# Scores of an attention layer from two-part float32r operands in two halves of the array's rows, in a schedule of sixteen like steps

## The reference

```python
x = x + 0.5 * ffn(layernorm(x))
x = x + attention(layernorm(x))
x = x + 0.5 * ffn(layernorm(x))

# attention: 16 heads of 16 columns, over the 512 rows of a batch
q, k, v = x @ Wq + bq, x @ Wk + bk, x @ Wv + bv
q, k = rope(q), rope(k)
scores = einsum('bhqd,bhkd->bhqk', qh, kh) / sqrt(16)
out = einsum('bhqk,bhkd->bhqd', softmax(scores), vh)
return out @ W0 + b0

# ffn: base layer, eight autoencoders (256 -> 64 -> 256), and the adapter
# (256 -> 64 -> 256) that belongs to the autoencoder with the smallest loss on this batch
h = relu(x @ W_enc[n] + b_enc[n]); recon = h @ W_dec[n] + b_dec[n]
top1 = argmin_n mean((recon - x) ** 2)
return x @ W_base + b_base + adapter[top1](x)
```

## Time and profile before

| | us |
|---|---|
| median of 3 runs | 1968.64 (1968.19 to 1973.37) |
| profiled execution | 1970.23 |
| its span | 1968.4 |
| TensorE busy | 1812.3 (92%) |
| VectorE busy | 1270.6 (65%) |
| ScalarE busy | 986.5 (50%) |
| GpSimd busy | 503.9 (26%) |

### The profile page before, as it was taken

The page is one execution under the profiler, slowest core; times in us unless marked ns, Lnnn a source line. Parts: engine busy times, 40 slices in busy tenths (PEclk is TensorE's granted clock), DMA queues, the critical chain, the costliest instruction groups (busy, mean ns, idle before and its releaser), DMA issues.

```text
span 1968.4 us, 26397 instructions
## 1 busy us (share of the span) xinstructions
PE 1812.3 (92%) x9128; PEld 988.0 (50%) x9128; DVE 1270.6 (65%) x2795; ACT 986.5 (50%) x1954; POOL 503.9 (26%) x663
## 2 busy tenths in 40 slices
PE   6598999999999999999999999999999999998885
PEld 5343545454554645455454545545454554545244
DVE  5476776667666766666676676666667666674631
ACT  1245564545555455555545555564555545454541
POOL 1404132141412214141221414122141412213101
PEclk9698999999999999999999999999999999999897
DMA  4513215060320506032050603206050320505000
GB/s 110 91 17 70 39 28 91 12 108 6 64 51 26 94 12 108 4 71 46 27 93 12 108 4 70 47 21 98 12 108 2 67 52 20 100 1 105 4 12 11
DMA packets 96781, 99.40 MB, mean 50 GB/s; under 512 B 19975, under 2 KB 88328, under 8 KB 96520
## 3 DMA queue, kind: packets, MB, share of 16 engines
q1 hardware_dynamic: 93896, 97.19, 26.7%
q10 hardware_dynamic: 2752, 0.54, 0.2%
HBM read 63.54 MB, written 33.55 MB: 49 GB/s over the span
## 4 chain that ended last, share of the span: by engine, by line
PE 61%; DVE 12%; DMA 12%; ACT 4%; SPq 4%; issue 4%; POOL 2%; POOLq 0%; ACTq 0%; DVEq 0%
PE ps L514 10%; PE ps L502 9%; PE ps L581 8%; PE ps L490 8%; DMA scratch<-parts 7%; DVE mx L832 6%; PE ps L560 6%; SPq L475 4%; PE ps L569 4%; DMA out_dram<-x 4%; PE ps L618 3%; PE ps L636 3%; ACT pr L716 2%; PE ps L621 2%; PE ps L681 2%
## 5 line engine op out<-in xcount | busy, mean ns | idle before, releaser
L832 DVE TENSOR_REDUCE mx<-ps 128x1 f32<-128x512 f32 x1024 | 653.5, 682 | 230.6 <-PE ps L490 229.6
L716 ACT ACTIVATE pr<-ps 128x512 f32<-128x512 f32 x1024 | 555.8, 598 | 292.0 <-PE ps L502 291.5
L490 PE MATMUL ps<-stack 96*128 96x512 bf16 x1024 | 326.1, 387 | 27.1 <-DVE mx L832 23.7
L502 PE MATMUL ps<-stack 98*128 98x512 bf16 x1024 | 323.2, 386 | 20.0 <-ACT pr L716 9.5
L514 PE MATMUL ps<-pr,va 128*32 128x512 f32 x2048 | 274.3, 608 | 4.6 <-ACT pr L716 4.6
L502 PEld LDWEIGHTS ps<-stack 98*128 98x128 bf16 x1024 | 77.5, 100 | 273.5 <-ACT pr L716 174.3
L771 ACT ACTIVATE h<-ps,benc 128x512 f32<-128x512 f32 x128 | 88.0, 687 | 216.2 <-PE ps L560 216.2
L490 PEld LDWEIGHTS ps<-stack 96*128 96x128 bf16 x1024 | 97.8, 98 | 187.8 <-DVE mx L832 91.7
L884 DVE SCALAR_TENSOR_TENSOR ps<-ps,wb,h 128x512 f32<-128x512 f32 x128 | 96.7, 755 | 140.7 <-PE ps L569 140.7
L1029 POOL TENSOR_SCALAR rs<-mv 128x4 f32<-128x4 f32 x48 | 11.6, 242 | 608.3 <-DVE mv L852 602.6
L581 PE MATMUL ps<-xh,w_dh 128*128 128x512 f32 x256 | 124.4, 486 | 9.2 <-DVE ps L884 6.7
(11 more groups left out here) (155 smaller groups left out, 2971.0 us busy)
## 6 DMA issues: line engine op xcount, KB each, us to landing
stack<-scratch SPq DMA_DIRECT2D x384, 128.0 KB, 4.5
scratch<-parts SPq DMA_DIRECT2D x64, 384.0 KB, 5.6
xin<-in_L_attn_x_dram SPq DMA_DIRECT2D x16, 512.0 KB, 3.8
out_dram<-x SPq DMA_DIRECT2D x16, 512.0 KB, 6.1
stack<-wu_mT SPq DMA_DIRECT2D x128, 4.0 KB, 1.7
cst<-in_const_dram SPq DMA_DIRECT2D x1, 1024.0 KB
raw<-in_L_ffn_W_dec_dram ACTq DMA_DIRECT2D x1, 512.0 KB, 5.7
pr<-in_L_ffn_W_enc_dram SPq DMA_DIRECT2D x2, 256.0 KB, 7.6
```

The source lines that it names most:

```text
L490: pe.matmul(bank1[:, t % 2, :], stack[b.odd][0][0:KB, hd, 128 * t:128 * t + 128], stack[b.odd][1][0:KB, hd, :], start=True, stop=True).the ...
L502: pe.matmul(bank2[:, a % 2, :], stack[b.odd][1][:, 4 * g + a, 128 * t:128 * t + 128], stack[b.odd][0][:, 4 * g + a, :], start=True, stop=T ...
L716: act.activation(pr[:, n % 2, a, :], bank2[:, a % 2, :], ACT.Exp, scale=SCALE).then_inc(ex_done.sem, 1)
L832: dve.tensor_reduce(mx[:, hd // 4 % 2, e:e + 1], bank1[:, t % 2, :], AX.X, ALU.max).then_inc(mx_done.sem, 1)
```

## The change

- **Operands.** q and k are split in two float32r parts (high and low) in place of three bf16 parts. A head has three blocks of 16 rows in place of six (48 rows, 50 with the maxima). The GpSimd step for the rest and the ScalarE step for the middle part are gone.
- **Two halves of the array.** Even heads stand in partitions 0 to 49 of the stack, odd heads in 64 to 113. A score matmul then uses one half of the array's rows only. The four score matmuls of a half step (two of line 552 for the maxima, two of line 565 with the maxima subtracted) are issued in turn: half 0, half 1, half 1, half 0.
- **One stack.** The stack is held once. A new step, lift, reads the scratch back: 12 transfers at a time, for two of the four blocks, once the batch before has no more use for that half of the heads. High and low parts go to the scratch apart (put_high, put_low).
- **Sixteen like steps.** An iteration has 16 steps of two halves, each with both kinds of scores; the second scores and pv of a batch run over into the next iteration (LAG = 5). Each half step has about one piece of dense work. The end of the second feed-forward (dn, up, store) stands in the iteration after the next. x1 is held three times, va twice; the squares, the whole transposed input and oT have buffers of their own. gr isn't cut in two any more. en steps stand one in a half step, where first two of them stood together.

```diff
-BLOCKS = 6
+BLOCKS = 3
 KB = BLOCKS * HD
-Q_PARTS = (0, 0, 1, 0, 2, 1)
-K_PARTS = (0, 1, 0, 2, 0, 1)
+HALF = 64
+Q_PARTS = (0, 1, 0)
+K_PARTS = (0, 0, 1)
...
+STEPS = 16
+LAG = 5
...
+    def attention(s, half):
+
+        shifted = (i, s - LAG) if s >= LAG else (p, s - LAG + STEPS)
...
+        if now or shifted: step("ss", i if now else None, s, shifted, half)
...
+    for t in range(2 * STEPS):
+        attention(t // 2, t % 2)
+        if old and t == 0: step("mt", p, 3)
+        if now and t in (8, 16, 24): step("mt", i, t // 8 - 1)
+        if now and t == 10:
+            step("lift", i, 2)
+            step("lift", i, 3)
+        if old: second_ffn(t)
+        if older: end_ffn(t)
...
-        parts = [sb(f"parts{k}", [128, 3, S], BF16) for k in range(2)]
-        stack = [[sb(f"stack{o}{a}", [KB + 2, H, S], BF16) for a in range(2)] for o in range(2)]
+        parts = [sb(f"parts{k}", [128, S], FR) for k in range(3)]
+        stack = [sb(f"stack{a}", [128, H // 2, S], FR) for a in range(2)]
...
+            def spread(b, k, part):
+
+                for j, p in enumerate((Q_PARTS, K_PARTS)[k % 2]):
+                    if p == part:
+                        for e in range(2):
+                            sp.dma_start(stack[k % 2][HALF * e + HD * j:HALF * e + HD * j + HD, 4 * (k // 2):4 * (k // 2) + 4, :].bitcast(F32),
+                                         scratch[b.odd][k].rearrange("(h e) d a n -> e d h a n", e=2)[e, :, :, part, :])\
+                                .then_inc(stacked[k].sem, 16)
+
+            def lift(b, k):
+
+                sp.wait_ge(*ex_done.at(b - 1, H * T * (k // 2 + 1) // 2 - 1))
+                sp.sem_inc(passed, 1)
+                sp.wait_ge(*hi_put[k].at(b, 0))
+                spread(b, k, 0)
+                sp.wait_ge(*lo_put[k].at(b, 0))
+                spread(b, k, 1)
...
+            def maximum_scores(b, m, e):
+
+                p, t = divmod(m, T)
...
+                q = slice(HALF * e, HALF * e + KB)
+                pe.wait_ge(*mx_done.at(b, 2 * m + e - 2))
+                pe.matmul(bank1[:, e, :], stack[0][q, p, 128 * t:128 * t + 128], stack[1][q, p, :],
+                          start=True, stop=True).then_inc(s1_full.sem, 1)
+
+            def shifted_scores(b, n, half, x):
...
+                p, e = 2 * g + half, 1 - x
+                q = slice(HALF * e, HALF * e + KB + 2)
+                pe.wait_ge(*ex_done.at(b, 4 * n + 2 * half + x - 2))
+                pe.matmul(bank2[:, x, :], stack[1][q, p, 128 * t:128 * t + 128], stack[0][q, p, :],
+                          start=True, stop=True).then_inc(s2_full.sem, 1)
+
+            def scores(b, s, shifted, half):
+
+                for x in range(2):
+                    if b:
+                        maximum_scores(b, 2 * s + half, x)
+                    if shifted:
+                        shifted_scores(*shifted, half, x)
```

More of the change, by code:

```diff
@@ L113, in step @@
             do[name](*args)
-    def dense(s, half):
-        at = (s, half)
-        if new and at == (0, 0):
+    def attention(s, half):
+        shifted = (i, s - LAG) if s >= LAG else (p, s - LAG + STEPS)
+        if not 0 <= shifted[0].number < B:
+            shifted = None
+        if now or shifted: step("ss", i if now else None, s, shifted, half)
+        if shifted: step("s2", *shifted, half)
+        if now:
+            step("s1", i, s, half)
+            if s % 4 == 3 and half: step("ms", i, s // 4)
+        for b, m in ((i, s), (p, s + STEPS)):
+            if not 0 <= b.number < B:
+                continue
+            if LAG < m <= LAG + STEPS and half == (m < LAG + STEPS): step("pv", b, m - LAG - 1)
@@ new lines, in end_ffn @@
+    def end_ffn(t):
+        if t == 3: step("dn", pp, 1)
+        if t == 9: step("up", pp, 1, 0)
+        if t == 10:
+            step("up", pp, 1, 1)
+            step("store", pp)
+    for t in range(2 * STEPS):
[7 more added lines that the diff above has]
+        if older: end_ffn(t)
+        if new:
+            first_ffn(t)
+            queries(t)
@@ L210, in dense @@
-        if at == (23, 1):
-            if now: step("ot", i)
-            if load:
+            if t == 31:
                 step("tr", i + 2, 0, 0)
                 step("tr", i + 2, 0, 1)
-    for s in range(24):
-        for half in (0, 1):
-            if now:
-                if 5 <= s < 21: step("s2", i, s - 5, half)
-                if s < 16: step("s1", i, s, half)
-                if s in (3, 7, 11, 15) and half: step("ms", i, s // 4)
-                if 6 <= s < 22 and half == (s < 21): step("pv", i, s - 6)
-            dense(s, half)
@@ L232, in enter, with walk @@
             do[name](first, *args)
-def walk(engine, do):
-    def one(i, number, odd):
-        schedule(do, Batch(number, odd), now=0 <= i < B, old=1 <= i <= B, new=i + 1 < B, load=i + 2 < B)
-    def known(i):
-        one(i, i, i)
-    for i in range(-1, B + 1):
-        known(i)
+def walk(do):
+    for number in range(-1, B + 2):
+        schedule(do, number)
 def macaron(nc, x_in, Wq, bq, Wk, bk, Wv, bv, W0, b0, W_base, b_base, W_enc, b_enc, W_dec, b_dec, W_down, b_down,
@@ L478, in _, with put_high @@
-            walk(sp, dict(load=load, store=store, mt=maxima, ro3=stack_up))
-            sp.wait_ge(*stored.at(Batch(B - 1, 1), 0))
+                for e in range(2):
+                    sp.dma_start(stack[0][HALF * e + KB:HALF * e + KB + 2, 2 * g:2 * g + 2, :]
+                                 .rearrange("n a (t k) -> n (a t) k", k=128).bitcast(F32),
+                                 mT[16 * e:16 * e + 16, g % 2, :].bitcast(F32)).then_inc(mq_done[g % 2].sem, 16)
+            def put_high(b, k):
+                sp.wait_ge(*hi_done.at(b, k))
+                sp.dma_start(scratch[b.odd][k][:, :, 0, :].rearrange("h d n -> (h d) n"), parts[HI_SLOT[k]][:].bitcast(F32))\
+                    .then_inc(hi_put[k].sem, 16)
@@ L481, in _ @@
+            def lift(b, k):
[5 more added lines that the diff above has]
+                spread(b, k, 1)
+            walk(dict(load=load, store=store, mt=maxima, ro2=put_high, ro3=put_low, lift=lift))
+            sp.wait_ge(*stored.at(Batch(B - 1), 0))
         @block.tensor
         def _(pe):
-            def s1(b, hd, half):
-                if half == 0 and hd % 8 == 0:
-                    pe.wait_ge(*stacked[2 * (hd // 8)].at(b, 0))
-                    pe.wait_ge(*stacked[2 * (hd // 8) + 1].at(b, 0))
-                for t in range(2 * half, 2 * half + 2):
-                    pe.wait_ge(*mx_done.at(b, T * hd + t - 2))
-                    pe.matmul(bank1[:, t % 2, :], stack[b.odd][0][0:KB, hd, 128 * t:128 * t + 128],
-                              stack[b.odd][1][0:KB, hd, :], start=True, stop=True).then_inc(s1_full.sem, 1)
@@ L683, in out_project @@
                 last.then_inc(op_full.sem, 1)
-            do = dict(s1=s1, s2=s2, pv=pv, mt=maxima, tr=transposed, en=encode, gr=gram, cost=cost, dn=down,
+            do = dict(ss=scores, pv=pv, mt=maxima, tr=transposed, en=encode, gr=gram, cost=cost, dn=down,
                           up=up, qk=project, va=values, nt=natural, ot=out_transposed, op=out_project)
```

465 lines of the change are left out of this document (233 added, 232 removed), and 3 rows, old and new, of the table QK.

## The result

The changed kernel takes 2094.24 us (median of 4 runs, 2090.33 to 2098.35); the kernel before took 1968.41 us beside it. The ratio is 1.0636, with a 95% interval of 1.0601 to 1.067: 6.4% slower, where 1826 us were forecast. The execution that was profiled took 2090.33 us, with a span of 2088.5.

The account below looks back on a forecast made before the run. TensorE was taken as the bound. Cheaper scores (7.4 us) and fewer stalls (1.5) save 8.9 us per iteration, 142 us over 16, from the profiled 1970.2 to 1828, or 1826 for the median; range 1750 to 1915.

Parts of the forecast that it names:

- What scores cost afterwards: TensorE's four score matmuls per half step: 0.64 us in place of 0.87, gaining 7.4 us per iteration (1.9 to 12.8).
- each change of mode empties the array: Rival: two drains and exposed loads make each half step's score group 1.04 us, 2031 us in all; chance 0.06.
- What stalls become: TensorE's idle time per iteration: 4.0 us go and 2.5 come, so -1.5 us (between +2.5 and -4.0).
- One wait grows: TensorE's wait at half step 0's encoder, behind the transposes of batch i+2, becomes about 2.5 us.
- The clock: Granted clock below full in mid-span, from sparser TensorE use, would make the forecast wrong altogether; not in the sum.
- The one stack: SyncE's twelve reads into the stack take 9.8 us of a near 20 us window, costing nothing; rival of lateness, chance 0.05.
- The first rival: Row halves don't run together: a half step's four score matmuls take 1.10 us, 2063 us in all; chance 0.14.
- Another engine takes over: Rival: VectorE's row maxima or ScalarE's exponents hold TensorE back, stalls grow by 6 us, 1946 us; chance 0.07.

Follow-up runs that it names:

- the run with three moves: Changed kernel with batch i+2's transposes, first feed-forward's dn and up, and second feed-forward's encoder steps moved to other half steps: 1949.93 us, ratio 0.9892.
- the run in one half: Changed kernel with the odd heads' scores replaced by the even heads', so all score matmuls use one row half: 2231.24 us, ratio 1.1323.
- the filler: Changed kernel plus unused float32r matmuls, 18 ahead of dn's wait and 12 ahead of the first q projection's: 2059.09 us, ratio 1.0432.
- the earlier transposes: Changed kernel with the transposes of batch i+2 in half steps 29 and 30 in place of 31 and 0: 2036.91 us, ratio 1.0329.
- all rows: Changed kernel with each score matmul over all 128 rows, both heads together, so scores are not those of a head: 2079.44 us, ratio 1.0552.
- the better order: Changed kernel with transposes, dn, up and second feed-forward's encoder steps moved: 1949.93 us with half-row scores, 1984.27 us with scores over all 128 rows.

## Why the prediction was wrong

The forecast was a period of 105.7 us, 8.9 less than before; it was 123.0, 8.4 more. Three terms make up the 8.4, from the window of the changed kernel and the full-clock iteration of the run with three moves: TensorE's work at the full clock, 106.3 less 110.3, is -3.9 us; the lower clock adds 110.6 less 106.3, +4.3; idle time adds +8.1. For the first point below, pv in the timeline of the kernel before, with a float32r matmul behind it:

```profile
1043.24 0.61 PE L502 MATMUL ps<-stack 98*128 98x512 bf16 x2
...
1044.21 1.07 PE L514 MATMUL ps<-pr,va 128*32 128x512 f32 x8
1045.21 0.49 PE L560 MATMUL ps<-xh,w_eh 128*128 128x512 f32 x1
1045.54 0.40 PE L560 MATMUL ps<-xh,w_el 128*128 128x512 f32 x1
```

- **What scores cost afterwards: failed.** The step was "For going in and out I have 0 below (bf16 to float32r costs nothing in rows 3) and 0.34 above ... I take the middle, 0.17". It is 0.40, outside my bounds. The two turns of 0.47 and the side-by-side halves were right (the run in one half). Pv's 0.22 was no fair row: its loads have 32 columns, and I read it where bf16 stands behind it. Where a float32r matmul does, that one takes 0.33 us in place of 0.233 in the kernel before too (1045.21 to 1045.54). There pv costs 1.20 us (1043.24 to 1045.54, less 0.87 and 0.233), and its price over 0.86 is 0.34. The rival "each change of mode empties the array", with 0.06, comes nearest to what was seen, a price at each end, and had 0.29 there where 0.20 was measured. Work at the full clock did fall by 3.9 us, but not in the gram stretches. Part of it is pv, which now costs 1.00 (the stretch with pv is 4.13, 950.56 to 954.69) in place of 1.08 or 1.20: between 16 x 0.08 = 1.3 and 16 x 0.20 = 3.2 us. Where the rest lies wasn't located.
- **What stalls become: failed.** The step was "I count the other 4.0 us as gone" together with "One wait grows", so -1.5 in all. The waits of before that it names did go (0.97 for pv's copy, 0.44 for va), but not one wait grew, five did. The one wait that I worked out came as I had it: 2.69 us where 2.5 was forecast, "for VectorE's subtraction, and behind it ScalarE". Four other chains I did not work out in the same way: en of the second feed-forward (3.0), dn (2.3), the q projection (1.7), mt's copy ahead of an encoder (1.1). Each has a chain of passes on ScalarE, VectorE or GpSimd, and by the table of half steps at most one half step of cover (up1 10 to dn 11, tr 17 to qk0 18, tr1 21 to en0 22, mt and en in 24). GpSimd's copies ahead of dn, which the prediction doesn't mention, wait for the other feed-forward's up, which shares their buffer and now stands in the half step ahead of dn: VectorE's sum (line 982) ends at 965.92, the first copy starts at 966.81 and dn at 968.14.
- **The clock: left out.** The text named it as what would make it "wrong altogether", and put no price on it. It is 4.3 us per iteration, half as much again as the idle time alone. That idle time has a part in it is shown by the filler (35 us faster with more work) and by the earlier transposes (19.7 us less busy time with the same matmuls). It is not the whole cause: over the whole run the six kinds of wait sum to 188 us in the changed kernel, 147 with all rows and 117 in one half, and the granted clocks are 0.921, 0.967 and 0.921. What else the clock follows stays open.
- **The one stack: right.** Twelve reads are issued in 5.48 us (5.3 forecast), the median read lands 6.0 us after its issue (4.5 assumed), and no wait for a transfer into the stack is among TensorE's waits of the iteration.
- **The first rival (halves don't run together): out**, by the run in one half. **Another engine takes over:** VectorE is at 60% and not the bound. But longer waits of TensorE for other engines, the size of which that rival put at +6 us, are what came: +8.1. That rival's 1946 lies outside the stated range of 1750 to 1915, though the text says that the range reaches over it.

## What to carry to other kernels

Before a reordering that spreads dense work, list every chain that leaves TensorE and comes back (transpose, passes on other engines, next matmul) and compare its length with the work left between its ends; one such sum for each chain, not for the worst alone. Add a price for the clock behind such waits: here it was 4.3 us for 12.4 us of idle time in an iteration. A packed group pays for the way in and out, 0.20 us at each end, and a group of four matmuls of 512 columns saves only 0.46 by packing. Compare it with the format that it replaces (0.87 us for bf16 here) and not only with its own unpacked form.

## What the hardware showed that I had not expected

- The two halves of the rows behave as two queues: a matmul starts ahead of an earlier one in the program if its half is free (933.94, both of L552 together).
- Going from full-row float32r or float32 matmuls to half-row ones and back costs 0.40 us, 0.20 at each end.
- The same wait of 1.6 us, with the same wait of 1.42 us ahead of it, was followed by the full clock in one iteration and by the lower level in another. What decides between them stays open.
- With the scores over all rows the mean granted clock was 0.967, with the same count and columns in one half 0.921, in kernels with waits of like length (1.68 and 1.61 us ahead of the second feed-forward's encoder). In the better order it was 0.980 with all rows and 0.955 with the halves. No run here says why.
